# A Mamba-style block on one Trainium2 core: in the first 24 blocks ScalarE takes the conv input and the oldest tap ahead of the conv silu

## The reference, cut to what matters

```python
xz = x @ W_in
x_proj, z = jnp.split(xz, 2, axis=-1)
xc = jax.lax.conv_general_dilated(x_proj.transpose(0, 2, 1), conv_w, ..., feature_group_count=D_INNER)
x_conv = silu((xc + conv_b[None, :, None]).transpose(0, 2, 1))
ssm = x_conv @ W_xproj
delta = jax.nn.softplus(ssm[..., 0])
deltaB = delta[..., None] * ssm[..., 1:1 + D_STATE]
h_mean = jnp.einsum('bld,bln->bdn', x_conv, deltaB) / L
y = jnp.einsum('bdn,bln->bld', h_mean, Cm) + D[None, None, :] * x_conv
attn = (y * silu(z)) @ W_out
x = _layernorm(x + attn)
x = _layernorm(x + fp4_linear(silu(fp4_linear(x, w_gate)) * fp4_linear(x, w_up), w_down))
```

## Time and profile before

| | |
|---|---|
| median of 3 executions | 1904.06 us (1903.47 to 1905.06) |
| the profiled execution | 1903.5 us, of which the span from first to last instruction is 1901.5 us |
| PE busy | 1823.6 us (96%) |
| PE weight loads | 1518.4 us (80%) |
| DVE busy | 1571.0 us (83%) |
| ACT busy | 1265.9 us (67%) |
| POOL busy | 1096.1 us (58%) |
| mean granted clock of TensorE | 0.989 of full |

### The profile page before, as it was taken

The page is one execution under the profiler, slowest core; times in us unless marked ns, Lnnn a source line. Parts: engine busy times, 40 slices in busy tenths (PEclk is TensorE's granted clock), DMA queues, the critical chain, the costliest instruction groups (busy, mean ns, idle before and its releaser), DMA issues. The chain is left out here.

```text
span 1901.5 us, 34283 instructions
## 1 busy us (share of the span) xinstructions
PE 1823.6 (96%) x10180; PEld 1518.4 (80%) x10180; DVE 1571.0 (83%) x3549; ACT 1265.9 (67%) x2617; POOL 1096.1 (58%) x1760
## 2 busy tenths in 40 slices
PE   6897999999999999999999999999999999899986
PEld 5665788888888888888888888888888888777775
DVE  5645788888888888988888888888889888888885
ACT  6776667677766767776676777667677766544443
POOL 3434465666666666666656666666566565555553
PEclk9899999999999999999999999999999999999998
DMA  5235232333332233333223332332333232122200
GB/s 175 95 107 170 92 104 93 108 103 117 100 112 103 94 107 104 119 98 114 100 97 105 107 115 98 114 102 98 106 106 112 102 99 94 63 81 70 76 31 17
DMA packets 120309, 190.60 MB, mean 100 GB/s; under 512 B 15040, under 2 KB 49728, under 8 KB 120128
## 3 DMA queue, kind: packets, MB, share of 16 engines
q1 hardware_dynamic: 120128, 188.42, 29.8%
HBM read 104.48 MB, written 83.89 MB: 99 GB/s over the span
## 5 line engine op out<-in xcount | busy, mean ns | idle before, releaser
L535 PE MATMUL pgu<-wgu_hi,xqT 128*128 128x512 f32 (+1 forms) x1536 | 416.4, 379 | 16.3 <-issue 15.0
L535 PEld LDWEIGHTS pgu<-wgu_hi,xqT 128*128 128x128 f32 x1536 | 279.7, 189 | 67.9 <-issue 18.8
L535 PE MATMUL pd<-wd_hi,hqT 128*128 128x256 f32 x1536 | 289.4, 287 | 5.2 <-DVE scratch L1225 2.0
L535 PEld LDWEIGHTS pd<-wd_hi,hqT 128*128 128x128 f32 x1536 | 237.6, 189 | 9.1 <-issue 4.7
L414 POOL TENSOR_SCALAR rs<-ssq 128x1 f32<-128x1 f32 x256 | 73.4, 287 | 286.5 <-issue 251.1
L1109 DVE SCALAR_TENSOR_TENSOR acc<-xps,cw,acc 128x512 f32<-128x512 f32 x256 | 200.3, 782 | 34.0 <-POOL acc L453 29.2
L535 PE MATMUL pgu<-wgu_lo,xqT 128*128 128x512 f32 (+1 forms) x768 | 227.4, 377 | 0.0
L1024 DVE SCALAR_TENSOR_TENSOR scratch<-scratch 128x256 f32<-128x256 f32 (+2 forms) x258 | 171.5, 665 | 61.7 <-ACT scratch L903 60.1
L805 ACT ACTIVATE scratch<-scratch,sum 128x256 f32<-128x256 f32 x256 | 130.2, 508 | 119.8 <-DVE scratch L1171 109.7
L611 PE MATMUL pd<-wout,g 128*128 128x256 f32 x864 | 204.0, 379 | 0.0
L416 POOL TENSOR_TENSOR rs<-rs,nhalf 128x1 f32<-128x1 f32 x256 | 178.6, 698 | 21.3
(11 more groups left out here) (142 smaller groups left out, 4447.6 us busy)
## 6 DMA issues: line engine op xcount, KB each, us to landing
sz_hbm<-szs SPq DMA_DIRECT2D x128, 256.0 KB, 2.0
xc_hbm<-xcs SPq DMA_DIRECT2D x128, 256.0 KB, 2.0
early<-xc_hbm SPq DMA_DIRECT2D x128, 256.0 KB, 2.7
early<-sz_hbm SPq DMA_DIRECT2D x128, 256.0 KB, 3.0
xin<-in_x_t_dram SPq DMA_DIRECT2D x32, 512.0 KB, 4.7
xres<-in_L_attn_x_dram SPq DMA_DIRECT2D x128, 128.0 KB, 2.3
out_dram<-scratch SPq DMA_DIRECT2D x128, 128.0 KB, 1.7
early<-in_L_attn_W_in_dram SPq DMA_DIRECT2D x2, 512.0 KB, 4.7
```

The source lines that it names most:

```text
L535: mm = pe.matmul(bank, lhsT, rhs, start=(m == 0), stop=(m == len(pairs) - 1))
```

## The change

In the steps with g_ up to LAG, ACT runs conv_input and oldest_tap of block u before conv_silu of block v = u - 1, no longer after it. Every instruction and every wait stays as it was; step 0 has no conv_silu. The other engines' code is the same.

```diff
                     if g_ <= LAG:
+                        conv_input()
+                        oldest_tap()
                         if exists(v):
                             conv_silu()
-                        conv_input()
-                        oldest_tap()
                         z_silu()
                         weight_copies(u)
                         if exists(v):
```

## The result

The changed kernel takes 1915.43 us (median of 7, 1909.40 to 1918.88), the kernel before 1904.07 us (median of 7, 1903.47 to 1905.72): a ratio of 1.0051, 95% interval 1.0034 to 1.0068. A repetition (5 and 20 executions) gave 1915.72 against 1904.39 us, 1.0061 (1.0048 to 1.0073). So the change costs some 0.5 to 0.6%, where 0.13% was forecast. Not only the median moved: the seven executions of the changed kernel lie over 9.5 us, the seven of the kernel before over 2.3 us. Over the 20 executions of the repetition the kernel before spreads more, from 1903.04 to 1907.30 us.

The account below looks back on a forecast made before the run. Only the first 24 steps count, where ACT's silus wait for DVE's taps in a ring; later PE sets the pace. Starts summed to +2.4 us: 1903.5 + 2.4 = 1905.9, plus 0.56 for the median: 1906.5 us, range 1901.0 to 1910.5.

Parts of the forecast that it names:

- The taps' wait: First 24 steps: ACT's conv silus idle 34.4 us waiting for DVE's middle taps; the change was to remove this wait.
- the new ring: Silu, state_projection, x_product, conv_input, next silu in a plain step: 3.64 + 1.90 = 5.54 us, against 5.58 before.
- the sum: Starts written out for steps 1 to 23: state_projection of step 23 comes 2.4 us late, giving 1906.5 us; chance 0.42.
- the taps' slack: Steps with DVE and POOL weight work: the taps have some 2 us of slack, into which that work falls.
- The rival built on it: Steps 1 to 11: DVE passes hold up POOL's conv_sum through the shared port lock, +5.5 us, 1912.0 us; chance 0.12.
- 6.85: Length in us of a step at TensorE's lower clock, x_product 4.95 plus 1.90, against 5.55 before; used for step 5.
- the likeliest case: First 24 steps: the starts as written out hold, 1906.5 us; chance 0.42.
- at the lower clock again: Step 21, behind softplus: TensorE falls to its lower clock once more, so the step takes 6.9 us.
- The argument against it: PE's waits before state_projection grow to about 1.1 us in plain steps, nearer to the harmless 0.62 than to 4.00.
- The lower clock comes more often: Rival: x_product is in the closed chain of waits, two to three more falls at 1.3 us, 1909.1 to 1910.4; chance 0.16.
- the 171.0 of the sum: Forecast start in us of PE's state_projection in step 23, against 168.61 before.
- its +2.4: Forecast delay in us of step 23's state_projection, carried whole to the end: 1903.5 + 2.4 = 1905.9 us.

Follow-up runs that it names:

- the first trace: Profiled execution of the changed kernel, no further edit, against the kernel before: 1910.05 us, where the profiled execution before took 1903.5 us.
- the earlier trace: Profiled execution of the kernel before, nothing changed: 1903.5 us.
- run 5: Kernel before with the new order only in steps 0 to 11, the old one from step 12 on: 1906.30 us, 1.0006 against the kernel before.
- run 6: Kernel before with the new order only in steps 12 to 23, the old one in steps 0 to 11: 1913.12 us, 1.0052 against the kernel before.
- The second trace: Trace of another execution of the changed kernel, timed again without edit: 1915.72 us.
- run 2: Kernel before plus spare matmuls on PE ahead of state_projection in most of the first 24 steps: 1908.20 us, 1.0020 against the kernel before.
- runs 9 and 10: Three spare matmuls ahead of x_product in steps 2 to 23: kernel before 1907.80 us (+3.0), changed kernel 1924.36 us (8.6 above the changed kernel).
- Run 3: Changed kernel plus spare matmuls ahead of state_projection, 3 a step, 14 in steps 1, 5 and 21, none in 9, 13, 17: 1909.85 us; trace from 1912.45 us.
- the order by step: Kernel before, silu first behind softplus and in steps 19 and 23, else between conv_input and oldest_tap: 1901.01 us; with 12 spare matmuls in steps 5 and 21, 1897.60 us.

## Why the prediction was wrong

**Right: what bounds the stretch.** The taps' wait vanished, the new ring stood in its place, and its parts were read well. Step by step the sum and the first trace agree, all but step 2 at the full clock: step 2 7.06 and 7.08 us, step 4 9.54 and 9.55, step 6 5.8 and 5.70, step 12 8.2 and 8.19, step 13 6.3 and 6.37, step 18 9.3 and 9.37, step 20 8.17 and 8.18. Plain steps were a little longer than 5.54: 5.56 to 5.59. Step 7 was not read well, 5.9 and 6.38 us at the full clock: DVE's passes lay without a gap up to the taps, which ended at 65.66, and the silu waited 0.28 us for them.

**Right in the main: DVE and POOL.** But for that one wait the weight passes went into the taps' slack. In step 10 the collision of the earlier trace rows is still there:

```profile
82.19 2.82 POOL L401 TENSOR_TENSOR scratch<-g 128x1536 f32<-128x1536 f32 x1
...
82.72 3.63 DVE L1109 SCALAR_TENSOR_TENSOR acc<-xps,cw,acc 128x512 f32<-128x512 f32 x2
```

The taps took 3.63 us instead of 1.53, ended at 86.35, and the silu started on time at 86.44, 5.71 after the one before. The exclusive lock that the Trainium skill describes (SBUF — State Buffer, "SBUF: two separate sides") agrees with these rows, in which the two taps end 1.34 us after the product. The rival built on it fell in runs 5 and 6, since the half of the steps with the passes costs 1.7 us and the other 8.5.

**Wrong: the clock.** The step that failed is the one in which the cost of the lower clock was written out as "6.85" for step 5 and in which the likeliest case took steps 5 and 21 alone to be at the lower clock ("at the lower clock again" for 21). Two things were off. The size: the 6.85 left state_projection and the transposes at nearly their full speed; when the fall comes ahead of them, the ring takes 8.01 us, 2.4 more than at the full clock and not 1.3. The number: steps 3, 15, 24 and 27 fell too, in one execution or both. The argument against it was that waits of 1.1 us are nearer to the harmless 0.62 than to 4.00. It doesn't hold: ahead of step 15 PE waited 1.10 us in both traces, and the step ran at the full clock in one (6.01 us) and at 0.78 in the other (7.61). In the first trace the state_projection of step 23 came 3.1 us later than the 171.0 of the sum: 1.1 us in step 3, 1.2 in step 5, 0.3 in step 21 and, not by the clock, 0.4 in step 7; the rest is small and of both signs. Behind it came 1.6 us in step 27, of which other steps gave back 0.6. The second trace puts 3.6 us on top up to step 23 and 1.6 in step 24. The rival "The lower clock comes more often" was the right one. It had 0.16, at 1.3 us a fall, and ended at 1910.4, while five of the seven executions lay above that.

**Why the old order didn't show it.** There the clock fell in steps 2, 5, 7, 11 and 21 (granted 0.71, 0.69, 0.73, 0.52 and 0.74 from silu to silu) and steps 2, 5 and 7 lost nothing by it (5.81, 5.55 and 6.43 us; at the full clock step 2 took 5.82 and step 7 6.44 in run 6, step 5 5.56 in run 2), because x_product had the whole latency of POOL and DVE to finish in; runs 9 and 10 show the same with the clock left out. But the old order isn't free of it: the low clock of step 11 showed up in steps 12 and 13 (run 5), and over 20 executions the old order spreads over 4.3 us. I had read the old trace as a clock that costs nothing, and priced the falls of the new order by how often the old one had them.

**The parts of the loss.** An estimate of the new order at the full clock comes from the first trace, if its low steps are given the length that they have at the full clock (step 3 5.56 us, step 5 5.6, step 21 5.56). The silu of step 12 then comes at 89.0, 2.5 us earlier than the 91.44 of before, and that of step 24 at 172.4, 0.3 us later than 172.08. Run 3's trace says the same: its silu of step 24 came 3.67 us late, of which 2.2 are the spare matmuls of step 1 and 1.1 the low clock of step 5 (6.64 against 5.56), which leaves 0.4. So the order by itself gains in the first half nearly what it loses in the second, as the sum had it: its +2.4 less two falls of 1.3 is -0.2. By these traces nearly all of the median's 11 us is the clock: 5.1 us in steps 3, 5 and 21 and 1.6 in step 27 of the first trace, 5.2 more in the second. How they divide among the steps can't be told from medians, since each execution falls in other steps.

## What to carry to other kernels

An idle time on one engine that many steps share is the latency of a ring; before an instruction is moved out of it, write down the ring that remains and compare their lengths, as here 5.58 and 5.54 us. Then ask which engines are in the new ring: one whose speed varies, as TensorE's clock does here after waits, costs little outside of the ring (nothing in steps 2, 5 and 7 of the old order) and up to its whole slowdown inside (2.4 us in step 5 of the new one). And place the instruction step by step: the silu first where its input is long there (behind softplus), elsewhere behind conv_input alone, which frees the bank for the next block.

## What the runs showed that was not expected

Spare matmuls that compute nothing made a kernel faster twice: 1915.72 to 1909.85 us in the changed order, 1901.01 to 1897.60 us in the order by step. In the old order they made it slower, 1904.39 to 1908.20 us. In the changed order the granted clock of step 21 went from 0.76 and 0.57 to 1.00 by them. The Trainium skill (TensorE: Matmul & The Clock Gate, "What's actually happening") says that the slower clock is the default and that activity releases the faster one; these runs agree. And at the lower level, 1.2 GHz, the eight small matmuls of state_projection held the transposes up by 1.73 us instead of 0.92, so that this group of narrow matmuls slowed down as much as the wide ones (0.85 us from pair to pair of 512 columns instead of 0.46). In the second trace step 3 was low from its state_projection on and took 7.82 us, in the first only from x_product on, 6.63: one program, the same order, two lengths.
